# Two graph layers and two expert layers on one core: straight-line code, fp16 pairs for the first layer's sums, tiles of 256 nodes

## What is computed

```python
x = x + gnn0(layernorm(x), edge_weight1, W, b, src, dst)
x = x + ffn0(layernorm(x))            # 8 experts, 256 -> 512 -> 256, relu
x = x + gnn1(layernorm(x), edge_weight, Wp, bp, W1, b1, W2, b2, src, dst)
x = x + ffn1(layernorm(x))            # 8 experts, 256 -> 256 -> 256, gelu
# gnn0: agg = segment_sum(feat[src] * weight, dst) / max(degree, 1); [agg, feat] @ W.T + b
# gnn1: h = relu(x @ Wp.T + bp); agg = sqrt(segment_sum(h[src]**2, dst)); h @ W1.T + b1 + agg @ W2.T + b2
```

## Time and profile before

| | us |
|---|---|
| median of 3 runs (3587.98 to 3589.01) | 3588.11 |
| span of the profiled execution | 3152.2 |
| what lies around the span | 435.9 |
| TensorE matmuls busy | 2668.3 (85%) |
| VectorE, GpSimd, ScalarE busy | 1761.0, 1701.2, 1099.0 |
| gathers issued | 1680 |

### The profile page before, as it was taken

How to read it: one execution, slowest core, us unless ns; L and a number is a source line. 1 busy time by engine, 2 the same in 40 slices (tenths; PEclk the granted TensorE clock), 3 DMA queues, 4 the chain that set the end, 5 groups by cost and what they waited for, 6 DMA issues and landing times.

```text
span 3152.2 us, 46968 instructions
## 1 busy us (share of the span) xinstructions
PE 2668.3 (85%) x15708; PEld 1661.9 (53%) x15708; DVE 1761.0 (56%) x4216; ACT 1099.0 (35%) x1692; POOL 1701.2 (54%) x1793
## 2 busy tenths in 40 slices
PE   0368999999999999999999993468888888888888
PEld 0366566565665666656656542344444444444444
DVE  4644656556566565565655644345555655555555
ACT  1122433334344343343333440123333433333334
POOL 0475364463553735537346005777777777777740
PEclk9998999999999999999999995579988999989989
DMA  7532232232322323224224003222222222222220
GB/s 227 157 99 84 62 108 68 72 102 62 98 78 67 112 62 88 81 63 116 60 81 91 6 17 108 58 59 59 64 59 66 65 64 64 65 64 65 64 37 13
DMA packets 89035, 239.08 MB, mean 76 GB/s; under 512 B 30121, under 2 KB 34489, under 8 KB 88175
## 3 DMA queue, kind: packets, MB, share of 16 engines
q0 software_dynamic: 67200, 165.26, 19.4%
q1 hardware_dynamic: 21615, 71.10, 7.7%
HBM read 210.51 MB, written 25.73 MB: 75 GB/s over the span
## 4 chain that ended last, share of the span: by engine, by line
PE 52%; POOL 23%; issue 12%; DVE 6%; DMA 4%; ACT 1%; SPq 1%; POOLq 0%; DVEq 0%; ACTq 0%
POOL ring L602 23%; PE psY L698 16%; PE psH L677 15%; PE psE L663 12%; PE psM L760 4%; DMA ring<-table,idx 3%; DMA xin<-x_in 1%; PE psM L714 1%; DVE hsc L1226 1%; PE psC L684 1%; DVE hid L1221 1%; ACT hid L1389 1%; DVE aggs L1107 1%; PE psM L722 1%; PE psM L774 1%
## 5 line engine op out<-in xcount | busy, mean ns | idle before, releaser
L602 POOL DMA_INDIRECT ring<-table,idx x1680 | 1672.2, 995 | 1049.0 <-PE psE L667 487.6
L663 PE MATMUL psE<-ohw,ring 128*128 128x40 f32 x5040 | 689.5, 297 | 386.8 <-DMA ring<-table,idx 374.5
L1389 ACT ACTIVATE hid<-psH,b,scl 128x484 f32<-128x484 f32 x624 | 470.5, 754 | 1355.3 <-PE psH L677 1354.2
L663 PEld LDWEIGHTS psE<-ohw,ring 128*128 128x128 f32 x5040 | 685.5, 211 | 472.8 <-issue 347.7
L698 PE MATMUL psY<-hsc,wbuf 128*128 128x484 f16 x3744 | 894.8, 375 | 33.2 <-DVE hsc L1226 32.7
L677 PE MATMUL psH<-xnT,wbuf 128*128 128x484 f16 x3744 | 902.8, 378 | 6.5 <-issue 6.5
L1221 DVE TENSOR_TENSOR hid<-hid,psC 128x484 f32<-128x484 f32 x624 | 410.3, 657 | 488.5 <-ACT hid L1389 404.6
L698 PEld LDWEIGHTS psY<-hsc,wbuf 128*128 128x128 f16 x3744 | 353.0, 99 | 469.7 <-DVE hsc L1226 68.6
L677 PEld LDWEIGHTS psH<-xnT,wbuf 128*128 128x128 f16 x3744 | 359.6, 103 | 341.2 <-issue 38.5
L1080 DVE TENSOR_TENSOR acc<-acc,psE 128x120 f32 (+1 forms) x420 | 99.6, 237 | 632.2 <-PE psE L663 312.0
L1226 DVE TENSOR_TENSOR hsc<-hid,hsc 128x484 f16<-128x484 f32 x624 | 410.1, 657 | 0.2
(11 more groups left out here) (136 smaller groups left out, 1638.8 us busy)
## 6 DMA issues: line engine op xcount, KB each, us to landing
ring<-table,idx POOLq DMA_INDIRECT x1680, 2.5
xin<-x_in SPq DMA_DIRECT2D x20, 484.0 KB
wbuf<-w_in SPq DMA_DIRECT2D x4, 2048.0 KB, 13.6
table<-res SPq DMA_DIRECT2D x13, 484.0 KB
feat<-table SPq DMA_DIRECT2D x13, 484.0 KB
x_d<-x SPq DMA_DIRECT2D x13, 484.0 KB
xin<-x_d SPq DMA_DIRECT2D x13, 484.0 KB
out_dram<-x SPq DMA_DIRECT2D x12, 484.0 KB
```

The source lines that it names most:

```text
L602: pool.indirect_dma_start(out=l.ring[:, k16 % l.R, k, :], out_offset=None, in_=l.table, in_offset=bass.IndirectOffsetOnAxis(ap=idx[:, k16, ...
L663: last = mm(psE[:, o + h * W:o + (h + 1) * W], l.ring[:, r, k, h * P:(h + 1) * P], ohw[:, q, k, :], start=(k == 0), stop=(k == SUB - 1))
L1389: f(hid[n % 4][:, :], psH[n % 2][:, 0:T], (ACT.Relu, ACT.Gelu)[l.i], scale=l.un_up, bias=l.b1[:, n // l.HC, n % l.HC:n % l.HC + 1]).then_i ...
```

## The change

The kernel is rewritten without loops over tiles, with blocks of 128 nodes. `Shape` cuts the 49 blocks into 24 tiles of two blocks (256 nodes) and one of one block; a tile's groups are those whose edges it needs, about 8.3 on average (208 in all), the first tile's 11. `plan` puts them at the steps. The order of the steps and the places of the other work in them are kept, with half the columns.

- Layer 0's table holds fp16 pairs of the normed x times 2^11 (same bytes a row); the edge weights are fp16 pairs too (`wpair`), the one-hots fp16. A group has 24 fp16 products and 4 with `ones_h`. `feat` is transposed by fp16 products with an identity.
- Gathers take their indices from `src_s` directly; there are no index copies.
- The table is made from x in seven loads of seven blocks, which lie where the expert weights go later; norm on VectorE and ScalarE, high part on ScalarE, low part on GpSimd. The weights are loaded after it.
- Blocks are contiguous rows now, so that take copies without a permutation, and acc is cleared by 256 columns.
- The first layer's split of the weights starts at group 7 (at_scales = 6), GpSimd's reduction for it stands before group 8.

```diff
-PT = 121
-T = SUB * PT
+T = SUB * P
...
+        self.B = [2] * (blocks // 2) + [1]
+        self.NT = len(self.B)
+        self.T = [b * P for b in self.B]
...
+        self.NG = -(-e // GE)
+        self.END = [min(self.NG, -(-((s + w) * e) // (n * GE)) + LAG) for s, w in zip(self.S, self.T)]
...
-    table0 = nc.dram_tensor("table0", (NPAD, D), F32, kind="Internal").ap()
+    table0 = nc.dram_tensor("table0", (NPAD, 2 * D), F16, kind="Internal").ap()
...
+            def plan(self):
...
+                for t in range(1, NT):
+                    gs = list(sh.groups(t))
+                    early = len(gs) * (self.M - self.turn) // self.M
+                    late = gs[early:]
+                    for k, g in enumerate(gs[:early]):
+                        if t == 1:
+                            self.begun[k * 4 // early].append(g)
+                        else:
+                            n = self.turn + k * (self.M - self.turn) // early
+                            steps[self.M * (t - 2) + n].append(g)
+                    for k, g in enumerate(late):
+                        steps[self.M * (t - 1) + k * self.at_take // len(late)].append(g)
...
+            for i in range(NX7):
+                pool.wait_ge(s_t0h, i + 1)
+                pool.tensor_tensor(stg[i % 2][:, :, D:2 * D], x0[:, i * XR:(i + 1) * XR, :],
+                                   stg[i % 2][:, :, 0:D], ALU.subtract).then_inc(s_t0l, 1)
...
+                    if l.i == 0:
+                        for h in range(KD):
+                            for k in range(SUB):
+                                for m, (x, y) in enumerate(PARTS):
+                                    c = x * D + h * P
+                                    mm(psE[:, o + h * W:o + (h + 1) * W], l.ring[:, r, k, c:c + P],
+                                       ohw0[:, q, k, y, :], start=(k == 0 and m == 0),
+                                       stop=(k == SUB - 1 and m == 2))
+                        for k in range(SUB):
+                            last = mm(psE[:, o + 2 * W:o + 3 * W], ones_h[:, :], oh0[:, q, k, :],
+                                      start=(k == 0), stop=(k == SUB - 1))
...
-                iteration(l, tile, Chain(pe, s_act), 0)
+                for t in range(NT):
+                    last = t == NT - 1
+                    for n in range(l.M):
```

More of the change, by code:

```diff
@@ L435, in _ @@
+            for i in range(NX7 - 2):
+                t0_store(i)
             for dst, s in (
@@ L542, in _ @@
                 seed_load(l, 0)
-                def tile(t, q, first, last, more):
+                for t in range(NT):
+                    last = t == NT - 1
                     if not last:
@@ L1287, in _ @@
                 begin(4)
-                for j in batch(l, -1, l.M, False, True)[1]:
-                    onehots(l, 1, j)
+                onehots(l, l.at(0, 0))
                 scale(l, 0, 0)
-                def tile(t, q, first, last, more):
+                for t in range(NT):
+                    last = t == NT - 1
                     taking = adding = weighing = None
```

1077 lines of the change are left out of this document (556 added, 521 removed).

## The result

| | before | after |
|---|---|---|
| median, us | 3588.05 (4 runs, 3581.69 to 3589.01) | 3749.42 (4 runs, 3747.03 to 3757.56) |
| ratio | | 1.047, 95% interval 1.044 to 1.050 |
| span of the profiled execution | 3152.2 | 3745.2 |
| that execution's own time | not known | 3747.03 |

The change made the kernel 4.7% slower; the forecast was 3557 us, 0.9% faster, with a range up to 3730. The last two lines of the table are the first clue. After's span lies 1.8 us under its own time. Before's lay 435.9 us under the median, and the two therefore cannot be of the same condition.

A forecast was written before the change was run, and what follows sets the result against it. TensorE was taken to bound layer 0 and GpSimd's gathers layer 1. Layer 0's end at 1928 us plus 1193 for layer 1 gave a span of 3121; with 435.9 around it, 3557 us, range 3400 to 3730.

The forecast's parts named there:

- first up-product: Start of layer 0: table from seven large loads, then weights and their split; 202 us, 60 earlier.
- step of two blocks of six: TensorE's up and down products of one expert step at 256 columns: 1.32 us.
- group of 28 products: Layer 0's group sums in 16-bit products on TensorE: 1.04 us a group, between 0.75 and 1.34, for 1.81 before.
- tile of layer 0: A 256-node tile: 59.4 us of TensorE content, 9.5 of stalls, 1.3 for the clock; 70.3 us, 66 to 74.
- layer 1's first up after its first gather: Wait at the change of layers, 11 + 8 groups instead of 18 + 15: 106 us instead of 184.
- tile of layer 1: A 256-node tile: 42.9 us at full clock, 44.5 at a clock near 0.91 (42 to 48); gathers need 41.6.
- around the span: Time by which the median exceeded the profiled span of before: 435.9 us, kept unchanged in the forecast.
- the chain is dearer: Slower rival: each stall may be 0.3 us longer; tiles of 74 and 48 us, +173, 3730 us; chance 0.27.
- gathers bound layer 1: Faster rival: 16-bit products at 0.027 us, stalls falling together; tiles of 66 and 41.6 us, 3384 us; chance 0.22.
- the hand schedule: One tile of each layer scheduled by hand, in order on each engine: TensorE stalls 9.5 us and 10 us.
- The floor rival: Slower rival: 16-bit group products stay at 0.055 us, a group 1.54; +100, 3657 us; chance 0.07.
- tiles of 256 take nearly all of the rewrite's gain back: Whole kernel: the rewrite is worth some 400 us, nearly all lost again to the smaller tiles.

The follow-up runs named there:

- quick: The kernel after, unchanged, run again in the condition where before takes 3147 us (3551 to 3605 in the slow one): 2983.4 us, ratio 0.948.
- the longer lookahead: The kernel after with up(n+3) for up(n+2) ahead of down(n), here also with one gather a group instead of four: 2856.4 us, ratio 0.797.
- the tapered tiles: The kernel after with eleven tiles of four blocks, then 2, 2 and 1, instead of tiles of two: 3489.3 us, ratio 0.970.
- the run of 56: 56 products of 40 columns beside gathers, in code put behind the last store of the kernel after; that whole kernel took 3981.8 us.
- bare runs: Back-to-back fp16 products put behind the last store of several kernels; behind before, 3356.2 and 3345.3 us in all.

## Why the prediction was wrong, point by point

| step | forecast | quick | recorded (slow) |
|---|---|---|---|
| first up-product | 202 | 201 | 204 |
| step of two blocks of six | 1.32 | 1.31 | 1.31 where not held |
| group of 28 products | 1.04 (0.75 to 1.34) | 0.70 | 0.70 |
| tile of layer 0 | 70.3 (66 to 74) | 65.9 | 85.2 |
| end of layer 0 | 1928 | 1822 | 2260 |
| layer 1's first up after its first gather | 106 | 101 | 142 |
| tile of layer 1 | 44.5 (42 to 48) | 43.4 | 56.3 |
| span | 3121 | 2981.6 | 3745.2 |
| around the span | 435.9 | 1.8 | 1.8 |

**The step that failed is the last line.** The prediction took "the median of 3588.1 is 435.9 above the profiled span; I keep that as it is". It was no constant around the span, but time inside it: the hold-up of TensorE's updates beside gathers, of which the profile of before, taken in the other condition, has no trace. It doesn't stay either: it went from 417 us, by spans, to 764, and these 764 us are all of the way from the quick span of 2981.6 to the recorded 3745.2. No rival had it, though the list of what would show the forecast wrong ends on "a difference outside the span", and the range ended 19 us too low. The rival *the chain is dearer* ended on 3730 for other reasons: its tiles of 74 and 48 us were never there without late updates.

**In the condition of the profile the sum was 139 us too long**, and the time is that of the rival *gathers bound layer 1*, whose span of 2948 (3384 less 435.9) is within 1.2% of it. Half of that is luck: its 66 us for layer 0 were met, but in layer 1 43.4 were measured for its 41.6, and the gathers are not what bounds it, since without three of four of them it is 42.5. The tiles of layer 0 are 4.4 us shorter than forecast, 106 us in all, those of layer 1 1.1, 26 us. In layer 0 a group has 0.70 us for 1.04, under the lower bound, since a product takes 0.025 us, a little under the 0.027 of the bf16 ones, and not the middle: 2.8 us a tile. (The difference between the middle and the lower bound is 0.29 us a group, 60 us for 208 groups and not the 30 of the prediction.) The other products took 3.1 us more than priced by columns: TensorE is busy 59.7 of 65.7 us where 56.6 were left. The clock is 1.00, which takes away 1.3. And the waits are 6.0 for 9.5. These stand where the hand schedule had them, before down at steps 3, 5, 16 and 28, but are shorter (after in the quick condition, one tile):

```profile
868.43 0.83 PE L675 MATMUL psY<-hsc,wbuf 128*128 128x256 f16 x6 [1.32 <-DVE hsc L1236]
...
872.78 0.83 PE L675 MATMUL psY<-hsc,wbuf 128*128 128x256 f16 x6 [0.86 <-DVE hsc L1236]
...
894.81 0.83 PE L675 MATMUL psY<-hsc,wbuf 128*128 128x256 f16 x6 [0.70 <-DVE hsc L1236]
...
918.70 0.83 PE L675 MATMUL psY<-hsc,wbuf 128*128 128x256 f16 x6 [0.80 <-DVE hsc L1236]
```

The steps 13 to 16 were to cost 1.6 us and cost 1.0, 19 to 22 were to cost 1.6 and cost 0.7, 24 to 29 were to cost 2.2 and cost about 1.4.

**Right** were the step, the start (201 for 202), the start of layer 1 (101 for 106), GpSimd's 1.25 us a gather, and the chain of layer 1: the hand schedule gave 42.9 us at full clock, and 42.5 was measured when the gathers no longer bound it. The floor rival is dead: no product of a group needs more than 0.025 us.

**Wrong in its reason** was that tiles of 256 take nearly all of the rewrite's gain back. They cost nothing against tiles of 512 where nothing is held up, and the rewrite is worth 167 us there and not 400. What sets 65 us a tile in layer 0 is in part open: the groups' products count (16 of 28 left out took 2.4 us off a tile), but with two thirds of the steps' products gone it is still 64.2 us, at a clock of 0.72, and with the longer lookahead 65.0. VectorE, busy 46 of 65.7 us with handovers to ScalarE in every step, is what no run took away.

**Open is what the hold-up is in the machine.** No run shows what chooses the condition. Every timed run here was a profiled one, so no run tells whether the hold-up would be there without recording. For the recording speaks that about half of the semaphore events are missing from the slow traces with all gathers.

The Trainium skill (DMA: Bandwidth & Descriptors, section Why a DMA increments its semaphore by 16 and not by 1) has each of the 16 DMA engines add one to the semaphore; the trace agrees, with 16 events a gather where all are recorded. One gather in four takes three quarters of these events away, and three quarters of the transfers with them, so that the runs do not tell the two apart.

The Trainium skill (NOTIFIC — the notification-queue block, section 7.1 Overflow: three behaviours, one of which stalls the engine) describes the unit that writes such records to memory: its inside holds the producers back rather than lose a record, and a full ring of records in memory can, by its setting, drop new ones or stall the producer. The trace has something like both: TensorE is held back, and 18465 of 42805 semaphore events are missing. No run here shows that this is the path.

## What to carry to other kernels

Compare a profile's span with the time of the same execution before using it: here they differ by 1.8 us, and a gap of 436 was a second condition, not an overhead to carry along. A wait "remote" on a single core was a late semaphore update here; look whether it stands beside gathers, and compare the start of the waiting engine with the end of the product. Where that is found, fewer gathers and fewer, wider steps are worth more than the quick trace says: the tiling with half the columns is equal to tiles of 512 in one condition and, by the ratios to before (1.047, and 0.970 for the tapered tiles), 8% dearer in the other.

## What the runs showed of the hardware

- TensorE's semaphore updates came up to 11 us after the product in the kernel after, once 29 us in the kernel before, and 33 us in the run of 56, whose last products came late too and where the gathers, which waited for nothing, kept their pace of 1.25 us. All of this stood beside gathers: 448 products in 13.0 us alone had the usual lag, as had 28 beside gathers.
- The same chip was met in both conditions within the hour: before took 3147 and 3570 us on chip 8, 3144 and 3559 on chip 6.
- The lower granted clock came behind the hold-up: 1.00 from 1149 to 1156 us, in which TensorE fell idle, and 0.50 from 1157 to 1163; over the whole kernel it was 0.97 where three of four gathers were gone.
- A product of 128 weight columns and 40 columns of data in fp16 takes 25 ns in the kernel (24 in 0.60 us) and 27 to 34 ns in bare runs that start at a granted clock of 0.50.
- Leaving out two thirds of the steps' products gained 10 us of 2983: the granted clock fell to 0.72 in layer 0 and 0.56 in layer 1, and the step's chain stayed.
